# Raw weights loaded before the attention phase ends, two norms spread over three units, and a scan that starts six ticks earlier

## The reference

```python
x = _layernorm(x + attn(x))        # lightning attention, 16 heads, chunks of 128, per-head decay, gated head RMS norm
x = _layernorm(x + ffn0(x))        # silu(x W1') * (x W3'), Walsh-Hadamard over 2,048 hidden, then W2'
x = _layernorm(x + scan(x))        # selective scan, 512 channels x 32 states, y = scan(x) + x*D
x = _layernorm(x + ffn1(x))        # silu(gate) * up, hidden 2,048, then down
```

```python
deltaBC = einsum('bld,od->blo', x, W_bc)                 # rank 64, B 32, C 32
delta = softplus(deltaBC[..., :64] @ W_dt.T + b_dt)
def step(h, inp):                                        # over 512 positions of each of 4 sequences
    h = exp(delta_t[:, :, None] * A) * h + (delta_t * u_t)[:, :, None] * B_t[:, None, :]
    y_t = einsum('bdn,bn->bd', h, C_t)
```

## Time and profile before

| | |
|---|---|
| median of 3 runs | 1928.1 us (1927.26 to 1929.54) |
| profiled execution, device time | 1931.71 us |
| its span, first to last instruction | 1929.9 us |
| TensorE busy | 1781.0 us (92%) |
| VectorE busy | 1336.6 us (69%) |
| GpSimd busy | 1276.2 us (66%) |
| ScalarE busy | 988.4 us (51%) |
| granted TensorE clock, mean | 0.982 |

### The profile page before, as it was taken

One profiled execution on the slowest core, in us unless ns is written; L12 is line 12 of the kernel. 1 busy time (PEld: TensorE's weight loads), 2 busy tenths in 40 slices (PEclk: granted clock), 3 DMA queues, 4 the chain that ended last, 5 costly groups with the idle time before them and its releaser, 6 DMA issues. The chain is left out here.

```text
span 1929.9 us, 27715 instructions
## 1 busy us (share of the span) xinstructions
PE 1781.0 (92%) x9472; PEld 1140.3 (59%) x9472; DVE 1336.6 (69%) x1665; ACT 988.4 (51%) x1671; POOL 1276.2 (66%) x987
## 2 busy tenths in 40 slices
PE   7898998679998999999899899998999999999998
PEld 5666666447855556555455455554556555566886
DVE  2525244232228999889998999889999999994222
ACT  5444342465455656565566455565665555443212
POOL 4533542137518998879887988789988898893111
PEclk9999999889999999999999999999999999999999
DMA  7342332358947888678677887667788677774653
GB/s 240 127 142 72 121 117 82 134 197 291 327 137 276 304 269 295 229 256 282 223 264 240 269 270 254 219 241 254 247 275 276 236 259 260 274 252 145 207 193 99
DMA packets 159292, 427.37 MB, mean 221 GB/s; under 512 B 30992, under 2 KB 54160, under 8 KB 158768
## 3 DMA queue, kind: packets, MB, share of 16 engines
q1 hardware_dynamic: 159152, 425.60, 65.6%
HBM read 356.34 MB, written 69.21 MB: 220 GB/s over the span
## 5 line engine op out<-in xcount | busy, mean ns | idle before, releaser
L1796 POOL TENSOR_TENSOR h_times_c<-h_states,c_rep 128x512 f32<-128x512 f32 x512 | 666.8, 1316 | 115.3 <-DVE h_states L1699 69.6
L1553 ACT ACTIVATE decay<-delta_on_states,a_neg 128x512 f32<-128x512 f32 x512 | 353.5, 692 | 364.6 <-DVE h_states L1699 339.1
L1762 POOL TENSOR_TENSOR h_lo<-silu_in_h_lo,h_hi 128x512 fp32r<-128x512 f32 x128 | 167.2, 1306 | 209.7 <-ACT h_hi L1463 209.1
L1679 DVE TENSOR_TENSOR d_b<-du_spread,b_rep 128x512 f32<-128x512 f32 x384 | 256.7, 668 | 24.4 <-PE du_spread L1386 23.5
L84 PE MATMUL gate<-x_hi,w 128*128 128x512 f32 x512 | 245.7, 480 | 16.4 <-DVE w L1631 6.9
L1699 DVE TENSOR_TENSOR_SCAN h_states<-decay,h_last,d_b 128x512 f32<-128x512 f32 x192 | 245.6, 1279 | 9.2 <-ACT decay L1553 2.3
L1699 DVE TENSOR_TENSOR_SCAN h_states<-decay,d_b 128x512 f32<-128x512 f32 x192 | 234.0, 1219 | 18.0 <-ACT decay L1553 11.8
L84 PE MATMUL up<-x_hi,w 128*128 128x512 f32 x512 | 241.4, 472 | 1.4 <-DVE silu_in_h_lo L1642 1.4
L1386 PE MATMUL du_spread<-stack,selectors 96*128 96x512 bf16 x512 | 201.5, 394 | 43.1 <-DVE d_b L1679 32.3
L84 PE MATMUL y_or_aux<-h_hi,w 128*128 128x512 f32 x468 | 221.0, 472 | 8.6 <-POOL h_lo L1762 6.7
L1636 DVE SCALAR_TENSOR_TENSOR silu_in_h_lo<-silu_in_h_lo,gate 128x512 f32<-128x512 f32 x128 | 87.1, 680 | 172.0 <-ACT silu_in_h_lo L1459 171.9
(11 more groups left out here) (221 smaller groups left out, 3134.8 us busy)
## 6 DMA issues: line engine op xcount, KB each, us to landing
w<-w_split SPq DMA_DIRECT2D x336, 512.0 KB, 4.3
delta_on_states<-delta SPq DMA_DIRECT2D x256, 512.0 KB, 5.5
w_split<-w_presplit_hi_lo SPq DMA_DIRECT2D x32, 512.0 KB, 3.3
w_split<-w SPq DMA_DIRECT2D x16, 1024.0 KB, 7.3
w_presplit_hi_lo<-in_w13b SPq DMA_DIRECT2D x32, 256.0 KB, 3.6
h_times_c<-in_w13a SPq DMA_DIRECT2D x16, 512.0 KB, 4.4
w_split<-w_presplit SPq DMA_DIRECT2D x16, 512.0 KB, 5.3
delta_x_parts<-delta_x_parts_out SPq DMA_DIRECT2D x16, 384.0 KB, 4.9
```

Of the source, the lines that this page charges most:

```text
L1553: act.activation(da[:, s % ND], dring[:, s % NR], ACT.Exp, scale=a[:, column(s):column(s) + 1]).then_inc(s_da, 1)
L1679: dve.tensor_tensor(db[:, by_dve(s) % NB], uu[:, i % NU], brep[:, tile_of(s // SPO) % 2], ALU.mult).then_inc(s_db, 1)
L1762: pool.tensor_tensor(hl[:, idx % RH], sg[:, idx % RH], hh[:, idx % RH].bitcast(F32), ALU.subtract).then_inc(s_hl, 1)
L1796: pool.tensor_tensor(hc[:, s % NC_], hs[:, s % NH], crep[:, tile_of(s // SPO) % 2], ALU.mult).then_inc(s_hc, 1)
```

## The change

1. **First raw weights.** The tile that held q in the attention phase is allocated outside both phases; it holds q, then the raw gate and up weights, then part of the products with C. When the last tile's q has been used (decayed q made, all scores done), the attention phase's SP loads chunks 0 and 1 of the raw weights into it. The trunk no longer issues these two loads. ScalarE splits chunk 0 before x, VectorE takes the low part of the weights before those of x, and the first table load stands behind x's high part.
2. **Norms e = 0 and 1.** They stood at ticks 9 to 15 and 16 to 23, both in the first unit. Now e = 0 has ticks 8 to 21, e = 1 ticks 41 to 55. The split of tile 1's x goes from tick 36 to 84, since the squares use its place.
3. **Weights of pass 0.** `w13_high` and `w13_low` come first in their tick (the low part one tick earlier). The down weights stood every 6 ticks from 1 to 91; now at ticks 3, 9, 13, 18, then 1, 4, 9, 12 of each unit (last at 84), and their loads two ticks behind the use of the buffer, six ticks before the next use at the closest (eight before). The advance splits stood at 8, 30, 52, 74, 96, 118 and so on; now 34, 58, 66, 74, 82, 126 and so on.
4. **Chain to the scan.** For norms e = 2 and 13 (`AT_ONCE`) the table of Ln is loaded before the first square, and x is scaled in the tick of the inverse root. Rank 108 to 106, dt 110, 116, 118, 120 to 107, 109, 111, 112, states 112, 114 to 114, 115, softplus of the other three blocks 121 to 114, parts 113 to 109.
5. **Scan** from tick 118 over 536 ticks instead of 124 over 530: the same last tick. The second tile's preparation is moved 1 to 5 ticks forward with it. Norm e = 11 and the split behind it are two ticks earlier.

```diff
@@ attention, SP, after the last tile's loads
+                sp.wait_ge(s_qd, NT)
+                sp.wait_ge(s_sc, HPT * CPT * NT)
+                for i in range(2):
+                    sp.dma_start(qT[:, 2 * i:2 * i + 2], w13a[:, i]).then_inc(s_raw13[i], 16)
                 store_blocks(beside_chunks(NT))
@@ tables
-SCAN_TICK, SCAN_SPAN = 124, 530
+SCAN_TICK, SCAN_SPAN = 118, 536
-VAR_TICK = (12, 19, 105, 212, 283, 308, 404, 465, 500, 551, 596, 665, 692, 777)
+VAR_TICK = (19, 53, 105, 212, 283, 308, 404, 465, 500, 551, 596, 663, 692, 777)
-PRE_TICK = tuple(8 + 22 * i for i in range(NC))
+PRE_TICK = (34, 58, 66, 74, 82) + tuple(126 + 22 * i for i in range(NC - 5))
+W2_HIGH_AT = {PIECES * u + tick: HC * u + c for u in range(UNITS) for c, tick in enumerate((1, 4, 9, 12) if u else (3, 9, 13, 18))}
+RAW2_AT = {tick + 2: idx + 2 for tick, idx in W2_HIGH_AT.items() if idx + 2 < NC}
@@ trunk, SP
-                raw13_load(0)
-                raw13_load(1)
@@ trunk, ScalarE
                 def inverse_root(e):
-                    act.preload_act_table_set(LOG_EXP)
+                    if e not in AT_ONCE:
+                        act.preload_act_table_set(LOG_EXP)
                 def square(e, k):
+                    if k == 0 and e in AT_ONCE:
+                        act.preload_act_table_set(LOG_EXP)
-                act.preload_act_table_set(EXP_TANH)
                 for tick in range(FIRST_TICK, LAST_TICK):
                     s = step_at(tick)
+                    if tick in W13_HIGH_AT:
+                        w13_high(W13_HIGH_AT[tick])
                     if tick == FIRST_TICK:
+                        w13_high(0)
                         for k in range(KD):
                             x_high(0, k)
-                        w13_high(0)
+                        act.preload_act_table_set(EXP_TANH)
                         w13_high(1)
@@ trunk, VectorE
+                w13_low_of_first()
                 x_low_of_first()
-                w13_low_of_first()
```

More of the change, by code:

```diff
@@ L864 @@
 NORM_AT_END = (8, 10, 12, 13)
+AT_ONCE = (NORM_BEFORE_SCAN[0], NORM_AT_END[-1])
 ZERO_MEAN = NORM_BEFORE_SCAN + NORM_AT_END
@@ L1072, in trunk_phase @@
         s_bank = [p.sem(f"bank_taken{b}") for b in range(4)]
-        s_raw13 = [p.sem(f"raw13_in{b}") for b in range(2)]
         s_raw2 = [p.sem(f"raw2_in{b}") for b in range(2)]
@@ L1800, in _ @@
                     s = step_at(tick)
+                    if tick in W13_HIGH_AT:
+                        w13_low(W13_HIGH_AT[tick])
                     if s == -1:
@@ L1832, in program @@
         x = p.sb("x", [P, KD, TOK])
-        attention_phase(nc, x, en, cn, w13b, w13x, x_d, aw, ld_tok, ld_feat, ld_cols, wg1_d, wg2_d, nw_d, w2n, w2h)
-        trunk_phase(nc, x, w13a, w2h, w13x, w2b, sel_d, ysel_d, bsel_d, wall_d, wdt_d, fp_d, al_d, out)
+        first = p.sb("q_or_raw_or_h_times_c", [P, KD, TT])
+        s_raw13 = [p.sem(f"raw13_in{b}") for b in range(2)]
+        attention_phase(nc, x, first, w13a, s_raw13, en, cn, w13b, w13x, x_d, aw, ld_tok, ld_feat, ld_cols, wg1_d, wg2_d, nw_d, w2n, w2h)
+        trunk_phase(nc, x, first, s_raw13, w13a, w2h, w13x, w2b, sel_d, ysel_d, bsel_d, wall_d, wdt_d, fp_d, al_d, out)
 def kernel(**inputs):
```

60 lines of the change are left out of this document (28 added, 32 removed).

## The result

The changed kernel takes 1920.3 us (median of 6, 1917.08 to 1923.0), the kernel before 1931.3 in the same runs (1927.26 to 1935.77): ratio 0.9942, 95% interval 0.9926 to 0.9959. It is faster, by 11 us and not by 25.7, and lies outside the range of 1892 to 1914. The profiled execution took 1920.07 us.

What follows compares the result with a forecast made beforehand. TensorE was taken to bound ticks 24 to 103 and the stage behind the scan, TensorE and VectorE by turns the scan. Terms -2.9 -15.5 +2.4 -13.1 +5 -1.5 -0.1 = -25.7 us from 1928.1 gave 1902.4 us, range 1892 to 1914.

Steps and rivals of the forecast that it cites:

- The scan: Scan stage: six ticks moved into it cost 8.2 us if TensorE-bound, 2.0 if VectorE-bound; middle taken, +5 us.
- signs of being wrong: Forecast wrong if the scan stage is under 1156 or over 1165, or TensorE idles over 4 us between ticks 48 and 104.
- Start of the trunk: Gap before the first matmul: earlier raw weights bring the first matmul to 368.1, -2.9 us, bounds -2 to -3.
- First unit: Ticks 0 to 23: one norm instead of two, 35.6 us for 51.1, -15.5 us, bounds -22.5 and -9.
- Ticks 24 to 103: FFN ticks behind the first unit: denser transfers of packed advance splits carry over, +2.4 us, bounds 0 and +8.
- the rival: Ticks 24 to 103: transfers take back what the first units win, +8 instead of +2.4, 1908 us; chance 0.14.
- Chain to the scan: Tick 104 to first scan: reordered norm, rank and dt bring the first scan to +38, -13.1 us, bounds -16 and -8.
- Behind the scan: Stage after the scan: norm e = 11 two ticks earlier removes two waits, -1.5 us, bounds 0 and -2.
- The rival "slower": Second tile's preparation: dt order makes TensorE wait, 512 scan steps each lose 0.05 us, 1934 us; chance 0.03.
- The last norm: End of the kernel: with the table load moved, Ln gains a tenth at most, -0.1 us.

Runs made afterwards that it cites:

- norms_old: The changed kernel with norms e = 0 and 1 back at ticks 9 to 15 and 16 to 23, tile 1's split at tick 36: 1931.7 us.
- pre_early: The changed kernel with each advance split's raw down weights loaded right behind the store of the split before: 1914.3 us, ratio 0.9903.
- chain_old: The changed kernel with chain, first scan tick and both tiles' preparation as before the change: 1920.6 us.
- after: The changed kernel itself, scan from tick 118 over 536 ticks: 1920.3 us, ratio 0.9942 to the kernel before.
- scan124: The changed kernel with the scan from tick 124 over 530 ticks again, all else as changed: 1909.1 us, ratio 0.9891.
- less_pe: The changed kernel with early loads and scan from 124, leaving out the gate's third pass in 39 chunks (156 matmuls): 1908.7 us, ratio 0.9881.
- scan118_530: The changed kernel with the scan from tick 118 but over 530 ticks, ending at tick 648: 1918.7 us.
- scan124_prep: The changed kernel with the scan from tick 124 and the second tile's preparation at its old ticks: 1911.8 us, ratio 0.9900.
- scan127: The changed kernel with early loads and the scan from tick 127 over 527 ticks: 1909.5 us, ratio 0.9874.
- the third buffer: Third decay buffer in SBUF, decays issued two steps ahead, in the early-load kernels with scan from 124, 118, 122, 127: 2006.3, 2007.2, 2001.8, 1990.4 us.

## Why the prediction was wrong

The profiled executions differ by 11.6 us and not by 25.7. The scan is 12.5 us over its term and ticks 24 to 103 are 8.5 over theirs. Against that stand 2.8 us of an earlier end of attention, which nobody forecast and which is luck, 2.4 of the first unit and 1.7 behind the scan. Two of the prediction's own signs of being wrong came: the scan stage is over 1165, and TensorE was idle for 6.1 us between ticks 48 and 104, more than 4.

**Start of the trunk: right.** The gap is 4.1 us for 6.9, and the first matmul waits for x's low part as worked out.

**First unit: right, a little too cautious.** 33.2 us for a forecast of 35.6 and -17.9 for -15.5, of which the norms' spacing alone is 16.2 (norms_old). The term that was too large is the wait for centring and squares, forecast at 3.0 us idle and 1.7 at the lower clock: the wait was 1.37, and that for the mean's copy 0.93.

**Ticks 24 to 103: the rival was right.** The forecast said "slack of 6 to 10 ticks in most transfers" and took +2.4. The prediction did not ask for the slack of the advance splits' own loads: each is issued three ticks (4.1 us) before ScalarE needs it. Moving these loads alone gave back 7.2 of the 10.9 us. The other 3.7 are the second norm's, and its term was too small as well: in pre_early, at a clock of 1.00, TensorE is busy for 115.14 us, 6.3 more than the 108.8 of the FFN, where 4.4 were forecast for the groups of products, and idle for 1.9. The prediction's account of 113.3 us before, 108.8 and 2.7 of lower clock and a wait, leaves 1.8 without a name. The stated bound of +8 was too low: I had taken it from the stretch's bandwidth and not from the latest single load.

**Chain to the scan: right as a time, wrong as a gain.** The first step came after 37.9 us (38 forecast). But the sum booked these 13.1 us as if the end of the kernel moved with the first step. TensorE had been idle for 7.0 us in this stage, and is now for 3.6 (37.90 less 34.33): what was won for the TensorE-bound work of the FFN is 3.4 us. The other 9.7 are TensorE's work, busy 44.06 and now 34.33, which moved behind the first step. chain_old fits: with the chain and first tick of before, 104 to end is 1394.2, with the new ones 1395.5.

**The scan: the step that failed.** "Where TensorE is the bound they cost 6 x 1.36 = 8.2 us; where VectorE is, [...] 2.0. [...] I take the middle, +5 us." The stage is 17.5 us longer, more than twice the higher of these prices. 10.0 of it are TensorE busy for longer (34 matmuls more that the chain left over, 7.7 us at 1.36 for six, the rest at a clock of 0.98 for 0.99), of which the middle of two prices booked only half; 7.5 are more idle time of TensorE, for which the sum has no term at all. In its place the runs show a cost of the place: with the same tables otherwise and early loads, the scan from tick 118, 122, 124 and 127 gives ratios of 0.9903, 0.9943, 0.9871 and 0.9874. Tick 118 against 124 is worth 11.2 us by the medians (after against scan124). The prediction had read that both engines are busy to 94% and take turns, and yet priced the six ticks as if one or the other were the bound at each moment; less_pe shows that TensorE's own work is no such price.

**Behind the scan: right in kind.** -3.3 for -1.6.

**The rival "slower"** was mis-added: 512 steps of 0.05 us more are 26, which makes 1928 and not 1934.

**The last norm: right.** Ln of the changed kernel starts 0.04 us behind the end of the variance product, where the earlier trace rows show 0.13:

```profile
1910.55 1.12 PE L1336 MATMUL y_or_aux<-rstd,sum_weights_eps 128*128 128x512 f32 x2 [0.69 <-ACT rstd L1483]
1911.71 0.69 ACT L1489 ACTIVATE rstd<-y_or_aux,sum_weights_eps 128x512 f32<-128x512 f32 x1 [1.22 <-PE y_or_aux L1336]
```

The Trainium skill (ScalarE: Activation LUTs, What ACT_TABLE_LOAD costs) gives each switch about 1.38 us of drain besides the load, by which the prediction had estimated a gain of 1.5 us here. This trace doesn't bear it out: in the chain above, the copy of C starts 0.01 us behind the end of a table load (555.64 and 1.28, then 556.93).

**What stays open** is what makes a first tick good or bad, that is, what makes TensorE's waits longer with the same work. Not it are the length of ScalarE's softplus blocks (split in two at two places, no change), the spread of the steps (scan118_530) and the second tile's preparation (scan124_prep). The waits for ScalarE's copies go with 118 but not with 121 and 122. The decays were taken out of the waits, and the spread stayed, but in kernels 4% slower. Not tried were other ticks of the advance splits, and whether the clock that falls behind one wait brings on the next. That the order in which VectorE's and TensorE's queues hold steps and FFN pieces makes it is only argued. Single executions of one kernel also differ by up to 11 us (scan127: 1898.98 to 1909.94).

## What to carry to other kernels

Book a shorter chain by the idle time that it takes from the engine with the most work behind it, not by how much earlier its last step comes; here 13 us earlier took 3.4 us of idle time away. Compare two places of a loop over stages that hold the same work, and split the difference into idle time and time at the lower clock. A load that is issued right before its use has no slack, whatever the average rate: when splits or tiles are packed closer, move their loads first. Where two engines are both busy to over 90% and hand steps to each other, neither's busy time is a price: take work out of each in turn and measure, look at the clock beside the time, and try several places of a new loop, since two ticks made 17 us by the medians and 14 by the ratios.

## What the hardware showed that was not expected

- A scan with both inputs in SBUF took 1.77 us and not 1.28 beside GpSimd, but 1.22 to 1.28 in the six cases with GpSimd idle, and GpSimd's operations grew too: its product with C (into the tile that had held q) went from a mean of 1313 to 1403 ns, its low part of h from 1310 to 1467. The four kernels were 80 to 103 us slower than the same without the third buffer. The Trainium skill (SBUF — State Buffer, Who interferes with whom) says that a VectorE instruction with two SBUF inputs contends with a GpSimd instruction that reads SBUF; the traces agree, and the scans with their decay in PSUM stayed at 1.28 us in the same trace.
- Less work for TensorE can bring it a lower clock: 35.4 us less work, but 61.4 us of the scan at the lower level in place of 17.1, so 10.9 us less busy, 19.7 us more idle, and a scan 8.8 us longer in the profiled execution.
